# All edges of a two-layer graph kernel sorted in batches of three units, none gathered, with the ranks made two batches ahead

## The reference, cut to what matters

```python
h = relu(layernorm(x))
x = x + segment_sum((h * node_vec1)[src], dst) * node_vec1_n2                   # layer 0
h = relu(layernorm(x))
x = x + (1 + eps) * h + segment_sum(relu(h[src] + edge_attr_32), dst)           # layer 1
```

## Time and profile before

| | |
|---|---|
| median of 3 runs | 6152.03 us |
| the profiled execution, its time and span | 6146.08 us, span 6144.3 us |
| POOL busy | 4655.4 us (76%), 4404 instructions |
| DVE / PE / ACT busy | 3122.4 (51%) / 2601.4 (42%) / 1243.8 us (20%) |
| indirect DMAs: scatters / gathers of layer 0 / of layer 1 | 1875 / 1250 / 1250 |
| layer 0 from the first scatter to the turning of the sums (L1308) | 63.16 to 4288.37 us |
| layer 1 from the first source one-hot to the turning of the sums | 4336.99 to 6119.23 us |

### The profile page before, as it was taken

The page is one execution under the profiler, slowest core; times in us unless marked ns, Lnnn a source line. Parts: engine busy times, 40 slices in busy tenths (PEclk is TensorE's granted clock), DMA queues, the critical chain, the costliest instruction groups (busy, mean ns, idle before and its releaser), DMA issues.

```text
span 6144.3 us, 89788 instructions
## 1 busy us (share of the span) xinstructions
PE 2601.4 (42%) x32958; PEld 2184.0 (36%) x32958; DVE 3122.4 (51%) x8199; ACT 1243.8 (20%) x2303; POOL 4655.4 (76%) x4404
## 2 busy tenths in 40 slices
PE   0322333333222223333332322234577887787776
PEld 0312222222222112222222211123466676666665
DVE  6534444433443334444333433223787777877776
ACT  0201111111111001111111110011333333333332
POOL 5777777777777777777777777776677777777774
PEclk9756666666665556666666655566678777878887
DMA  4311222222222211222222222102111121111211
GB/s 83 75 34 27 46 46 46 46 46 46 45 46 46 46 27 34 46 46 46 47 46 45 45 46 45 26 16 55 37 49 47 48 60 47 50 47 47 60 47 25
DMA packets 442929, 278.32 MB, mean 45 GB/s; under 512 B 341686, under 2 KB 411686, under 8 KB 436086
## 3 DMA queue, kind: packets, MB, share of 16 engines
q1 hardware_dynamic: 300926, 183.48, 12.4%
q0 software_dynamic: 140000, 83.16, 7.9%
q10 hardware_dynamic: 1560, 5.60, 0.3%
HBM read 192.42 MB, written 79.52 MB: 44 GB/s over the span
## 4 chain that ended last, share of the span: by engine, by line
POOL 73%; issue 22%; DVE 3%; DMA 1%; PE 0%; SPq 0%; ACT 0%; POOLq 0%; DVEq 0%; ACTq 0%
POOL records L552 32%; POOL message L542 21%; POOL stage L542 20%; DVE arena L1132 1%; PE plain_ps L855 0%; DMA stage<-table,src_plain 0%; DMA xs<-in_x 0%; DMA stage<-in_edge_attr 0%; DVE arena L1120 0%; SPq L402 0%; DVE arena L1308 0%; DVE centered L1156 0%; DVE counts L1014 0%; DMA table<-centered 0%; DMA record<-records 0%
## 5 line engine op out<-in xcount | busy, mean ns | idle before, releaser
L552 POOL DMA_INDIRECT records<-stage,place_i x1875 | 1939.1, 1034 | 605.4 <-issue 571.4
L542 POOL DMA_INDIRECT stage<-table,src_plain x1250 | 1368.6, 1095 | 404.4 <-issue 379.1
L542 POOL DMA_INDIRECT message<-table,src_plain x1250 | 1320.0, 1056 | 380.9 <-issue 380.9
L1120 DVE TENSOR_SCALAR arena<-arena,row_key 125x1280 bf16<-125x1280 f16 x1000 | 525.3, 565 | 1731.9 <-ACT arena L657 1731.9
L801 PE MATMUL key_rows<-ident,record 128*125 128x128 f16 x5000 | 461.5, 250 | 1734.2 <-DMA record<-records 1660.0
L1132 DVE TENSOR_SCALAR arena<-window_iota,dst_rel 128x320 bf16<-128x320 f16 x5000 | 1167.7, 305 | 3.6
L801 PEld LDWEIGHTS key_rows<-ident,record 128*125 128x125 f16 x5000 | 424.3, 163 | 1773.3 <-issue 1350.7
L657 ACT ACTIVATE arena<-key_rows 125x640 f16<-125x640 f16 x1000 | 647.5, 703 | 1727.2 <-PE key_rows L801 1720.8
L838 PE MATMUL sorted_agg<-arena 128*96 128x320 bf16 x5000 | 924.7, 341 | 102.4 <-DVE arena L1132 101.1
L855 PE MATMUL plain_ps<-centered,message 128*96 128x128 bf16 x2500 | 577.1, 402 | 466.8 <-DMA message<-table,src_plain 457.5
L838 PEld LDWEIGHTS sorted_agg<-arena 128*96 128x96 bf16 x5000 | 661.5, 141 | 239.9 <-DVE arena L1132 136.8
(11 more groups left out here) (122 smaller groups left out, 2024.4 us busy)
## 6 DMA issues: line engine op xcount, KB each, us to landing
record<-records SPq DMA_DIRECT2D x50, 1650.0 KB, 7.4
stage<-in_edge_attr SPq DMA_DIRECT2D x125, 400.0 KB
records<-pad SPq DMA_DIRECT2D x25, 1650.0 KB
records<-stage,place_i POOLq DMA_INDIRECT x1875, 2.1
message<-table,src_plain POOLq DMA_INDIRECT x1250, 2.4
stage<-table,src_plain POOLq DMA_INDIRECT x1250
table<-parts ACTq DMA_DIRECT2D x4, 585.9 KB
xs<-in_x SPq DMA_DIRECT2D x4, 390.6 KB
```

Source lines behind the costliest of these rows:

```text
L542: pool.indirect_dma_start(message[:, k, j, :] if l == 0 else rows[:, k, j, :], None, table0 if l == 0 else table1, bass.IndirectOffsetOnAx ...
L552: pool.indirect_dma_start(records, bass.IndirectOffsetOnAxis(ap=place_i[:, h, e:e + 1], axis=0), stage[:, h, e, :], None).then_inc(scatter ...
L1120: nc.vector.tensor_scalar(src_onehot[:, g % 2, o, :], key_row[:, g % 2, :], row_key[0:NP, o:o + 1], None, ALU.is_equal).then_inc(src_oneho ...
```

## The change

All 125 units are sorted, in 42 batches of three (the last has two units). The gathers, the plain one-hots, products and sums are gone from both layers, and layer 1 has 42 batches to go through in place of 25. POOL's layer 0 is 3125 scatters. Further parts:

- DVE makes both ranks of batch b+2 in front of the one-hots of batch b.
- Scans are cut in halves, and most long instructions of the ranks are waited for before the next is issued. In layer 0 DVE also waits after each source one-hot and after every third destination one-hot of a group.
- Ranks are centred on 128, so that a bucket's lower half of destinations goes to its first tile and the upper half to its second. A tile's destination window is then 224 nodes wide, not 320: the first tile's from node 0 of the batch, the second's from node 96. Only the first one-hot of a batch is 320 wide.
- The start: a unit's lowest destination is read as its first (edges are sorted), so the first ranks do not wait for all destinations and the means of x; `center` of the first layer moves from POOL to DVE; SP loads batch 0 first.
- The prefix has nine matmuls in place of six; padding is copied in pieces of 10 tiles in place of 20; the windows' flag is made after the last batch.

```diff
-    PLAIN = 2
-    PER = SORTED + PLAIN
-    BATCHES = UNITS // PER
-    ROUNDS = (BATCHES - 4) // 2
+    BATCHES = -(-UNITS // SORTED)
+    LAST = UNITS - (BATCHES - 1) * SORTED
+    ROUNDS = (BATCHES - 6) // 2
+    WT = 224
+    UP = WA - WT
-    PAD = 20
+    PAD = 10
...
+        def dst_onehot(g, t):
+            room = dst_room[:, g % 2, 0:WA] if t == 0 else dst_room[:, g % 2, WA + (t - 1) * WT:WA + t * WT]
+            return room if g == 0 and t == 0 else room[:, 0:WT]
...
-            def step0(b, h, u):
-                if is_first(b):
-                    scatter(b, h, u)
-                if left_after(b) >= 1:
-                    scatter(b + 1, 1 - h, u + h)
...
-                for k in range(PLAIN):
-                    at_least(pool, plain_done[0], 2 * b - 1 + k if not is_first(b) else 0)
-                    gather(0, k, gathered[0][k], src_plain[:, h, k * J:(k + 1) * J])
-            over_batches(pool, step0)
+            over_batches(pool, scatter)
...
-            def step1(b, h, u):
-                for k in range(PLAIN):
-                    pool.wait_ge(plain_loaded[k], 32 * (b + 1))
-                    at_least(pool, plain_sum_ready, 2 * b - 1 + k if not is_first(b) else 0)
-                    gather(1, k, gathered[1][k], src_plain[:, k, 0:J])
-            over_batches(pool, step1)
...
                     for t in range(GROUP):
-                        last = nc.tensor.matmul(sorted_agg[h][0:WIDE, 0:WA], sorted_message[:, (2 * h + g) % MESSAGES, t, :],
-                                                dst_onehot[:, g % 2, t, :], start=(g == 0 and t == 0),
+                        into = agg if g == 0 and t == 0 else agg[:, up(b) * (t % 2):up(b) * (t % 2) + WT]
+                        last = nc.tensor.matmul(into, sorted_message[:, (2 * h + g) % MESSAGES, t, :],
+                                                dst_onehot(g, t), start=(g == 0 and t == 0),
...
-                for v in range(SORTED):
-                    last = nc.vector.tensor_tensor_scan(counts[:, v, :], not_first[:].rearrange("p g j -> p (g j)"),
-                                                        in_bucket[:, v, :], 0.0, ALU.mult, ALU.add)
+                for v in range(n):
+                    for some in (slice(0, BUCKETS * J // 2), slice(BUCKETS * J // 2, BUCKETS * J)):
+                        last = nc.vector.tensor_tensor_scan(counts[:, v, some], not_first[:].rearrange("p g j -> p (g j)")[:, some],
+                                                            in_bucket[:, v, some], 0.0, ALU.mult, ALU.add)
+                        if v < n - 1 or some.start == 0:
+                            step(last)
...
+                step(nc.vector.tensor_scalar(r, r, P + 0.25, TO_INTEGER, ALU.add, ALU.add))
+                step(nc.vector.tensor_scalar(r, r, TO_INTEGER, None, ALU.subtract))
...
+                step(nc.vector.scalar_tensor_tensor(tile_rel[:, 0:w], second[:, 0:w], -float(up(b)), rel, ALU.mult, ALU.add))
+                step(nc.vector.tensor_scalar(outside[:, 0:w], tile_rel[:, 0:w], float(WT), None, ALU.is_ge))
+                step(nc.vector.scalar_tensor_tensor(outside[:, 0:w], tile_rel[:, 0:w], 0.0, outside[:, 0:w], ALU.is_lt, ALU.max))
+                step(nc.vector.scalar_tensor_tensor(bad, r, 1.0, outside[:, 0:w], ALU.is_lt, ALU.max))
...
                     for o in range(2):
                         nc.vector.tensor_scalar(src_onehot[:, g % 2, o, :], key_row[:, g % 2, :], row_key[0:NP, o:o + 1],
                                                 None, ALU.is_equal).then_inc(src_onehot_ready[l], 1)
+                        if l == 0:
+                            dve.wait_ge(src_onehot_ready[l], 2 * nth + o + 1)
...
                     for t in range(GROUP):
                         tile = g * GROUP + t
-                        last = nc.vector.tensor_scalar(dst_onehot[:, g % 2, t, :], window_iota[:], dst_rel[:, h, tile:tile + 1],
+                        last = nc.vector.tensor_scalar(dst_onehot(g, t), window_iota[:, 0:WA if tile == 0 else WT], dst_rel[:, h, tile:tile + 1],
                                                        None, ALU.is_equal)
+                        if l == 0 and t % run == run - 1 and t < GROUP - 1:
+                            last.then_inc(dst_paused[l], 1)
+                            dve.wait_ge(dst_paused[l], nth * ((GROUP - 1) // run) + t // run + 1)
...
                 def step0(b, h, u):
-                    if left_after(b) >= 1:
-                        rank_all(b + 1, 1 - h, u + h)
                     if left_after(b) >= 2:
                         rank_within(b + 2, h, u + 1)
+                        rank_all(b + 2, h, u + 1)
```

More of the change, by code:

```diff
@@ L96, in gnn_two_layers @@
         before = sb("before", [P, P], F16)
-        ones = sb("ones", [P, P], F16)
+        halves = sb("halves", [P, P], F16)
+        less_halves = sb("less_halves", [P, P], F16)
         join32 = sb("join32", [WIDE, F])
@@ L491, in step1 @@
                 left = left_after(b)
-                if left >= 1:
-                    for k in range(PLAIN):
-                        sp_at_least(plain_message, 2 * b + k + 1)
-                        load_plain(b + 1, k)
                 if left >= 2:
@@ L510, in _ @@
             pool.memset(ident[:], 0.0).then_inc(pool_steps, 1)
-            pool.memset(before[:], 1.0).then_inc(pool_steps, 1)
+            pool.memset(before[:], 0.5).then_inc(pool_steps, 1)
             pool.iota(bucket_iota[:], pattern=[[1, BUCKETS], [0, J]], base=0, channel_multiplier=0,
@@ L518, in _ @@
             pool.memset(not_first[:, :, 0:1], 0.0).then_inc(consts_ready, 1)
-            pool.affine_select(out=before[:], in_=before[:], compare_op=ALU.is_ge, fill=0.0, base=-1,
+            pool.affine_select(out=before[:], in_=before[:], compare_op=ALU.is_ge, fill=-0.5, base=-1,
                                pattern=[[1, P]], channel_multiplier=-1).then_inc(consts_ready, 1)
-            pool.memset(ones[:], 1.0).then_inc(consts_ready, 1)
+            pool.memset(halves[:], 0.5).then_inc(consts_ready, 1)
+            pool.memset(less_halves[:], -0.5).then_inc(consts_ready, 1)
             pool.iota(batch_start[:], pattern=[[SLOTS, BATCHES]], base=-TILES, channel_multiplier=0,
@@ L779, in prefixes @@
                 pe.wait_ge(scans_ready, b + 1)
-                for v in range(SORTED):
-                    for w in range(v + 1):
-                        last = nc.tensor.matmul(prefix[:, v * BUCKETS:(v + 1) * BUCKETS], before[:] if w == v else ones[:],
-                                                counts[:, w, J - 1:BUCKETS * J:J], start=(w == 0), stop=(w == v))
+                n = units_in(b)
+                for v in range(n):
+                    for w in range(n):
+                        last = nc.tensor.matmul(prefix[:, v * BUCKETS:(v + 1) * BUCKETS],
+                                                before[:] if w == v else halves[:] if w < v else less_halves[:],
+                                                counts[:, w, J - 1:BUCKETS * J:J], start=(w == 0), stop=(w == n - 1))
                 last.then_inc(prefix_ready, 1)
-            pe.wait_ge(consts_ready, 4)
+            pe.wait_ge(consts_ready, 5)
             prefixes(0)
@@ L883, in step0 @@
                     over_groups(l, b, group)
-                    if not is_first(b):
-                        for k in range(PLAIN):
-                            plain_products(b - 1, k)
-                        for k in range(PLAIN):
-                            join_plain(b - 1, k)
                     join_sorted(b)
+                    if is_last(b):
+                        pe.wait_ge(most_ready, 1)
+                        nc.tensor.transpose(most_ps, most[:], ident[:]).then_inc(most_turned, 1)
                 def step1(b, h, u):
@@ L1012, in rank_within @@
-                step(last)
-                for v in range(SORTED):
-                    last = nc.vector.tensor_tensor_scan(counts[:, v, :], not_first[:].rearrange("p g j -> p (g j)"),
-                                                        in_bucket[:, v, :], 0.0, ALU.mult, ALU.add)
+                sources = src_sorted[:, h, 0:w]
+                step(nc.vector.tensor_scalar(scaled[:, 0:w], sources, 1.0 / C, 0.5 / C - 0.5, ALU.mult, ALU.add))
+                step(nc.vector.tensor_scalar(row_of[:, 0:w], scaled[:, 0:w], TO_INTEGER, TO_INTEGER, ALU.add, ALU.subtract))
@@ L1163, in add_window, with far_windows, add_sorted @@
-                def add_window(first, mask, width, joined, nth):
-                    if isinstance(nth, int) and nth == 0:
+                def far_windows():
+                    for j in range(J):
+                        last = nc.vector.tensor_scalar(far_onehots[:, j, :], window_iota[:, 0:WS], far_key[:, j:j + 1], None, ALU.is_equal)
+                    return last
+                def add_sorted(b):
+                    first = dve.value_load(local_i[0:1, bass.ds(b, 1)], min_val=0, max_val=QN - 1)
```

(2 more changed lines are left out.)

485 lines of the change are left out of this document (171 added, 314 removed).

## The result

The changed kernel takes 6061.79 us (median; 6060.94 to 6062.64) beside 6159.94 for the kernel before (6150.35 to 6169.1) in the same comparison: ratio 0.9841, 95% interval 0.9821 to 0.9861, 98 us less. A second comparison on another chip, in which the changed kernel ran as it is, gave 6075.11 beside 6151.15, ratio 0.9864 (0.9829 to 0.99). The forecast was 38 us less.

What follows compares the result with a forecast made beforehand. POOL's one queue of indirect DMAs was taken as the bound. 23 us from the start, in all 56 by the end of layer 0, less 18 in layer 1: 38 off 6152 gives 6114 us, range 5985 to 6250.

Steps and rivals of the forecast that it cites:

- The start: Before the first scatter: ranks of batch 0 no longer wait for all destinations and means; first scatter at 40, 23 us earlier.
- the half scans: POOL in layer 0: a scatter gets through once per half scan, a loss of 1.1 us per batch, bounds 0 and 4.8.
- of the remaining 4.4 I keep three quarters, 3.25: POOL in layer 0: loss per batch put down to the other rank steps and one-hots, 3.25 us kept, bounds 0 and 4.4.
- DVE's round: DVE's work per batch in layer 0: 83 of 99 us, so DVE waits for POOL and not POOL for DVE.
- The end of layer 0: From last scatter to L1308: 54 us, no longer covered by gathers; layer 0 ends at 4232 in place of 4288.
- Layer 1: DVE's 420 groups at 4.04 us plus other terms: 1800 us against 1782, 18 longer.
- G: Rival: edges fall out of the 224-wide windows and the far path runs, 7800 us more; chance 0.01.
- B: Rival: POOL goes nearly undisturbed in layer 0, 1.35 us per batch in place of 4.35, total 5989; chance 0.14.
- C: Rival: the narrower window buys nothing, DVE stays at 4.30 us per group in layer 1, total 6223; chance 0.13.
- D: Rival: disturbance stays as today, half scans holding POOL as long together as wholes, 180 us more, 6294; chance 0.09.
- F: Rival: DVE's round in layer 0 takes more than 99 us; at 4 over, 6282; chance 0.03.
- E: Rival: TensorE sets layer 1, its slow level all through at 4.57 us per group, 207 more, 6321; chance 0.05.

Runs made afterwards that it cites:

- the pieces in step: Changed kernel with scans, additions and multiplications of the ranks cut into pieces meant to take just over 1.263 us: 6016.91 beside 6166.47 (0.9757).
- the ranks behind: Changed kernel with the ranks made behind a batch's one-hots, not in front: 6064.67 beside 6155.72; on slow chips 8889.86 beside 8306.87, 8918.99 beside 8339.59.
- the two paused forms of the kernel before: Kernel before with pauses and half scans: 8490.74 beside 8339.59; paused, with scans and additions in step and plain one-hots in two pieces: 8505.75 beside 8353.04.

## Why the prediction was right in its sign and wrong in its size

- **The start** (23 us earlier): right, 39.96.
- **Layer 0 is POOL's queue of 3125 DMAs at 1.2624**: right; the scatters' stretch is 3945 + 162.
- **Disturbance, the half scans** (1.1 per batch): too low. 77.8 / 41.67 = 1.87. The mechanism (one scatter per piece) was right, and the difference to whole scans too (131 forecast, 130 measured): wholes cost 4.3 in the kernel before, as read, but 5.0 in the changed one. The halving that the prediction set beside the rule of the Trainium skill (SBUF — State Buffer, Who interferes with whom) would have given 2.1, which is nearer. The trace agrees with a hold to the end of an instruction, one scatter per half scan (1.495 us beside 1.496); that the loss halves with the length was the prediction's own step, and it is not borne out (5.0 whole, 1.87 in halves, 2.84 in quarters).
- **Disturbance, "of the remaining 4.4 I keep three quarters, 3.25"**: this is the step that failed. It was a choice with no row behind it, and it gave the pauses almost no worth. In the kernel before, the table gives these one-hots and rank steps 3.7 per batch, not 4.4. Measured, the one-hots cost (10.4 + 3.1) / 41.67 = 0.32 per batch and the ranks' additions, multiplications and bucket comparisons (27.1 + 26.7 + 8.0) / 41.67 = 1.48, together 1.8. That is 1.44 us by 41.67 batches, 60 us, less the 32 that the scans cost more: 28 of the 31 us. Without the pauses the one-hots cost 288.3 / 41.67 = 6.9 per batch, more than my upper bound of 4.4 for all of it, and the kernel was slower than before.
- **DVE's round** (83 of 99 us): right in what it decides, 12 us per batch to spare (forecast 16), POOL waits for nothing after the first scatter. The order of the ranks is free.
- **The end of layer 0** (54): 52.5.
- **Layer 1** (1800, group 4.04): 1790, group 4.01. The sum was near, but its terms erred both ways: 420 groups at 0.03 less are 13 us, the loop took 65 us of issue (line 1057) where I had 38, and little of the 16 for TensorE's slow level can have come at a granted clock of 0.96. The window is worth some 100 us, where the slope of the earlier trace rows gave 109.
- **Rivals**: G did not come: POOL has no instruction in layer 1 (x0). B was half right: the one-hots go free, the ranks do not. C, D and F are refuted by 1.95 us for ten one-hots, scatters of 1.2 us beside half scans, and POOL's 33.6 us of waiting. E too: the granted clock of layer 1 is 0.96, almost always the 2.4 GHz level, where before it was 0.79 and PE was busy for about the same share (1471.9 of 1789.9 us against 79%). The rule that the prediction set beside E (the Trainium skill, TensorE: Matmul & The Clock Gate, Part 1) agrees: fed by DVE without gaps, TensorE kept the upper level.
- The change's own idea, sorting all edges, adds no gain that the runs show: the DMAs are as many, the plain one-hots' 66 us go, but the ranks of two more units per five come, and layer 1 lasts 1790 in place of 1782. The kernel before with pauses and halves reaches 0.9801, the changed kernel 0.9841 and 0.9864.

Left open: why a DMA that touches both kinds of one-hots loses 0.69 us without pauses at 224 columns and only 0.14 at 320 in the kernel before (419 of them, 57.7 us); whether the pauses and the pieces in step add up in the kernel before.

## What to carry to other kernels

When a queue of short DMAs on POOL is the bound, look at each DMA's duration by what VectorE does beside it before moving work: here a few waits between VectorE's own instructions decide over 260 to 275 us, and the restructuring brought no gain beside them. Which instructions disturb has to be measured: here scans and one-hots do, the longer sums do not. Scans that ran beside such a queue did best in pieces that take a little more than one DMA does from start to start, and a finer cut was worse. A step moved to an idle engine can cost the first engine more than it saves: here 0.54 us on ten one-hots for a step of 0.40.

## What the hardware did that I had not expected

The scatters' step with DVE's scans, shown above: 1.287, 1.495, 1.688 and 2.793 us.

And the chips differ. On four chips (kernel before 8307 to 8353 us) TensorE nearly stands still in stretches in which POOL scatters: in the rows below one matmul every 1.4 to 4.2 us, idle for 1.1 to 3.9 before each, with nothing to wait for that the profile shows. From the changed kernel with the ranks behind, on such a chip, first the matmuls (0.26 us each), then POOL's group:

```profile
1386.49 0.26 PE L716 MATMUL key_rows<-ident,record 128*125 128x128 f16 x1 [2.54 <-issue]
1390.69 0.27 PE L716 MATMUL key_rows<-ident,record 128*125 128x128 f16 x1 [3.94 <-issue]
1392.09 0.27 PE L716 MATMUL key_rows<-ident,record 128*125 128x128 f16 x1 [1.13 <-issue]
1394.89 0.26 PE L716 MATMUL key_rows<-ident,record 128*125 128x128 f16 x1 [2.53 <-issue]
```

```profile
L515 POOL DMA_INDIRECT records<-stage,place_i x3125 | 3013.3, 964 | 3922.4 <-issue 2281.0 <-DVE key L943 1641.4
```

POOL's scatters are undisturbed there (0.964 us), but it waits 1641 us for ranks, as it would if scatters and TensorE's work followed each other. Every variant of the changed kernel is 4.5 to 9.5% slower than the kernel before on such a chip, the two paused forms of the kernel before 1.8 and 1.9%. What stops TensorE I could not tell, and the changed kernel itself did not run there. The gain of this change holds for the chips where the kernel before takes some 6150 us.
